# Head sums sent through DRAM and divided feature-major, and a norm in groups of 4 tiles, in a macaron transformer block

## What is computed

```
x = x + 0.5 * ffn(layernorm(x))
x = x + attn(layernorm(x))
x = x + 0.5 * ffn(layernorm(x))
# attn: q, k, v = split(x @ w_qkv.T), 16 heads of 16
probs = softmax(where(causal, q @ k.T / 4, lowest))
out = (probs @ v), heads side by side -> out @ w_out.T
# ffn: softmax of the gate over the tokens, top 2 of 8,
#      y = relu chain of w1, w2, w3; v[e] = sum of y * weight; out = chosen @ v
```

## Time and profile before

| what | before |
|---|---|
| median of 3 runs | 2114.99 us |
| lowest, highest | 2114.93 us, 2117.0 us |
| the profiled execution, its own time | 2126.23 us |
| its span in the profile | 2124.5 us |
| PE busy | 2047.7 us (96%) |
| PE's weight loads busy | 1584.0 us (75%) |
| DVE busy | 1817.7 us (86%) |
| ACT busy | 1598.6 us (75%) |
| POOL busy | 414.5 us (20%) |

### The profile page before, as it was taken

The page is one execution under the profiler, slowest core; times in us unless marked ns, Lnnn a source line. Parts: engine busy times, 40 slices in busy tenths (PEclk is TensorE's granted clock), DMA queues, the critical chain, the costliest instruction groups (busy, mean ns, idle before and its releaser), DMA issues.

```text
span 2124.5 us, 99858 instructions
## 1 busy us (share of the span) xinstructions
PE 2047.7 (96%) x43659; PEld 1584.0 (75%) x43659; DVE 1817.7 (86%) x4023; ACT 1598.6 (75%) x3311; POOL 414.5 (20%) x1118
## 2 busy tenths in 40 slices
PE   5899989999999999999999999999999999879998
PEld 3788866377877777777787777777778776658885
DVE  6666666899999999999999999999999994676665
ACT  5344446599999999999999999999999998334442
POOL 1333213411121111121111111111111111023330
PEclk8899989999999999999999999999999999979998
DMA  8211103300010000100001001000010002231112
GB/s 273 74 47 50 42 16 125 134 30 25 13 34 14 25 30 8 34 20 18 31 7 33 22 16 34 9 29 27 11 34 16 22 4 69 54 118 47 45 49 88
DMA packets 70394, 94.36 MB, mean 44 GB/s; under 512 B 16640, under 2 KB 59396, under 8 KB 69956
## 3 DMA queue, kind: packets, MB, share of 16 engines
q1 hardware_dynamic: 62796, 68.75, 10.1%
q0 software_dynamic: 6816, 19.20, 3.4%
q10 hardware_dynamic: 344, 0.01, 0.0%
HBM read 62.24 MB, written 25.43 MB: 41 GB/s over the span
## 4 chain that ended last, share of the span: by engine, by line
PE 88%; DVE 6%; issue 2%; ACT 1%; POOL 1%; DMA 1%; SPq 1%; another core or an unknown queue 0%; DVEq 0%; ACTq 0%; POOLq 0%
PE bank L1264 39%; PE bank L1257 22%; PE bank L1139 17%; PE bank L1346 3%; PE bank L1150 1%; PE bank L1375 1%; DVE stats L1405 1%; PE bank L1307 1%; PE bank L1157 1%; DVE rows L1427 1%; DVE x_res L1725 1%; SPq L698 0%; POOL work L591 0%; DVE work L1594 0%; PE bank L1217 0%
## 5 line engine op out<-in xcount | busy, mean ns | idle before, releaser
L966 ACT ACTIVATE feat<-bank 128x512 f32<-128x512 f32 (+3 forms) x2304 | 1263.2, 565 | 113.8 <-PE bank L1264 13.3
L1264 PE MATMUL bank<-work 96*32 96x512 bf16 (+2 forms) x15872 | 1206.4, 370 | 5.0 <-DVE work L1772 3.8
L1772 DVE TENSOR_REDUCE work<-bank 128x1 f32<-128x512 f32 (+1 forms) x1920 | 1178.9, 659 | 26.4 <-PE bank L1264 23.4
L1257 PE MATMUL bank<-feat,phase 128*17 128x128 f32 (+3 forms) x18432 | 879.2, 263 | 0.3 <-ACT feat L972 0.3
L1257 PEld LDWEIGHTS bank<-feat,phase 128*17 128x17 f32 x18432 | 588.4, 98 | 270.7 <-ACT feat L972 13.7
L1264 PEld LDWEIGHTS bank<-work 96*32 96x32 bf16 (+1 forms) x15872 | 472.6, 96 | 57.1 <-DVE work L1772 24.6
L1139 PE MATMUL bank<-work 128*128 128x256 f32 (+1 forms) x1872 | 398.4, 363 | 0.6 <-issue 0.2
L1139 PEld LDWEIGHTS bank<-work 128*128 128x128 f32 x1872 | 325.1, 192 | 37.1 <-issue 1.0
L625 POOL TENSOR_SCALAR_AFFINE_SELECT feat<-feat 128x128 f32<-128x128 f32 x512 | 145.1, 292 | 456.0 <-ACT feat L966 439.1
L1656 DVE COPY work<-phase 128x514 f32 x234 | 101.5, 436 | 124.1 <-ACT work L880 99.5
L578 POOL DMA_INDIRECT work<-token_table,row_no x142 | 138.1, 973 | 299.0 <-PE bank L1150 142.6
(11 more groups left out here) (201 smaller groups left out, 1371.9 us busy)
## 6 DMA issues: line engine op xcount, KB each, us to landing
phase<-in_w SPq DMA_DIRECT2D x12, 1024.0 KB, 12.0
work<-qk_parts SPq DMA_DIRECT2D x60, 192.0 KB
token_table<-rows SPq DMA_DIRECT2D x8, 1056.0 KB, 8.7
work<-work SPq DMA_DIRECT2D x512, 0.5 KB
qk_parts<-phase SPq DMA_DIRECT2D x20, 384.0 KB, 2.8
work<-qk_parts SPq DMA_DIRECT2D x60, 128.0 KB
qk_parts<-work SPq DMA_DIRECT2D x12, 384.0 KB, 2.8
x_res<-in_x SPq DMA_DIRECT2D x8, 512.0 KB
```

What stands on the lines that cost most here:

```text
L966: eng.activation(p_ring[:, n % P_RING, lo:QB], s_bank("probs", n)[:, lo:QB], ACT.Exp, scale=HD ** -0.5).then_inc(sig.s_done, 1)
L1257: mm = eng.matmul(bank[ACC_BANK][GRID * g:GRID * g + VW, GRID * i0:P], v_aug[:, t, h, :], weights[:, i0:TPJ, g, :], start=(t == 0), stop=( ...
L1264: mm = eng.matmul(out[GRID * g:GRID * (g + 1), width], left[:, GRID * g:GRID * (g + 1)], right, start=start, stop=stop)
L1772: eng.tensor_reduce(maxima[:, h % 2, j, PLACE[i], at:at + 1], scores[:, 0:hi - lo], AX_X, ALU.max).then_inc(sig.a_done, 1)
```

## The change

What ACT copied out of the PSUM bank is no longer transposed by DVE. SP stores it in DRAM (`head_sums`, [head, row, token]). When 8 heads of a query block are there (heads 7 and 15), five steps follow: SP loads the sums of 8 heads by 512 tokens as 128 by 32 ("load_totals"), DVE takes their reciprocals, SP stores them and loads both the 128 features by 512 tokens and the reciprocals, each spread over its head's 16 rows ("load_parts"), and DVE multiplies 128 by 512 ("divide"). `heads` is now feature-major, as the projection wants it, so the transpositions of heads (L1359) and ACT's copies (L980) are gone. The norm behind attention goes in groups of 4 tiles instead of 8. For the last unit, reciprocals and divide stand inside the projection's loop. The input's tokens are ordered otherwise on the host, and ACT's copies of the norm before attention undo that. The rows of the third norm lie in `work` instead of `rows`, the one-hot tensors of the second routing in `rows`, and three waits move: the load of the experts' weights waits for the last division, `acc` for the store of two units ago, and the staging of weights for the second table's store.

```diff
-LN_GRP = (4, 4, GRP)
+LN_GRP = (4, 4, 4)
...
+HEADS_PER_PART = P // HD
+TOTALS = HEADS_PER_PART * QB // P
...
-PV_LAG, PV_PAUSE, TURN_LAG, DIVIDE_LAG = 5, 1, 2, 2
+PV_LAG, PV_PAUSE, STORE_LAG = 5, 1, 2
+LAST_RECIPROCALS, LAST_DIVIDE = 8, 16
+DIVIDE_STEPS = (("load_totals", 7), ("reciprocals", 14), ("store_reciprocals", 16), ("load_parts", 21), ("divide", 30))
...
-        while unturned and unturned[0][0] <= n:
-            yield "turn", unturned[0][1]
-            undivided.append((n + DIVIDE_LAG, unturned.pop(0)[1]))
...
-                unturned.append((n + TURN_LAG, h * NJ + j))
+                later.append((n + STORE_LAG, "store_sums", h * NJ + j))
+                if h % HEADS_PER_PART == HEADS_PER_PART - 1:
+                    later += [(n + lag, what, h * NJ + j) for what, lag in DIVIDE_STEPS]
+                later.sort()
...
-        while undivided and undivided[0][0] <= n:
-            yield "divide", undivided.pop(0)[1]
+        while later and later[0][0] <= n:
+            yield later.pop(0)[1:]
...
+        sums_dram = nc.dram_tensor("head_sums", (H, GRID, S), F32).ap()
+        recips_dram = nc.dram_tensor("head_reciprocals", (H, S), F32).ap()
...
-        heads = rows[:, :, 0:D]
+        heads = rows[:, :, :].rearrange("p i r -> p (i r)")[:, 0:KD * S].rearrange("p (k s) -> p k s", k=KD)
+        late_rows = work[:, 0:NT * ROW].rearrange("p (i r) -> p i r", i=NT)
+        def rows_of(f):
+            return late_rows if f else rows
+        def summed_of(h, j):
+            return heads[:, h // HEADS_PER_PART, j * QB:(j + 1) * QB]
+        def recips_of(h, j):
+            return recips[j] if h // HEADS_PER_PART else heads[:, 1, j * QB:(j + 1) * QB]
+        def units_of(h, j):
+            return slice(h - HEADS_PER_PART + 1, h + 1), slice(j * QB, (j + 1) * QB)
+        def divisions(h, j):
+            return h // HEADS_PER_PART * NJ + j + 1
+        def of_parity(h, j):
+            return h // HEADS_PER_PART * NJ // 2 + j // 2 + 1
...
-                    elif what == "divide":
-                        h, j = UNITS[n]
-                        need.wait_ge(sig.recip, n + 1)
-                        eng.tensor_tensor(heads[:, TPJ * j:TPJ * (j + 1), h * HD:(h + 1) * HD], sums[:, n % 2, :, 0:HD],
-                                          bc(recip[:, n % 2, :], 2, [P, TPJ, HD]), ALU.mult).then_inc(sig.divided, 1)
...
                 if f == 1:
                     need.wait_ge(sig.pv, PV_ALL)
+                    need.wait_ge(sig.divided, KD * NJ)
...
+                elif what == "store_sums":
+                    h, j = UNITS[n]
+                    need.wait_ge(sig.acc, n + 1)
+                    eng.dma_start(sums_dram[h, :, j * QB:(j + 1) * QB].rearrange("w (g c) -> g w c", g=TPJ),
+                                  acc_out[:, n % 2, :]).then_inc(sig.sums_stored[n % 2], 16)
+                elif what == "load_totals":
+                    h, j = UNITS[n]
+                    heads_of, tokens = units_of(h, j)
+                    need.wait_ge(sig.sums_stored[n % 2], 16 * (n // 2 + 1))
+                    eng.dma_start(totals[:, j % 2, :], sums_dram[heads_of, HD, tokens]).then_inc(sig.totals_loaded[j % 2], 16)
+                elif what == "store_reciprocals":
+                    h, j = UNITS[n]
+                    heads_of, tokens = units_of(h, j)
+                    need.wait_ge(sig.recip, divisions(h, j))
+                    eng.dma_start(recips_dram[heads_of, tokens], totals[:, j % 2, :]).then_inc(sig.recips_stored[j % 2], 16)
+                elif what == "load_parts":
+                    h, j = UNITS[n]
+                    heads_of, tokens = units_of(h, j)
+                    need.wait_ge(sig.recips_stored[j % 2], 16 * of_parity(h, j))
+                    if h >= HEADS_PER_PART:
+                        need.wait_ge(sig.divided, divisions(h - HEADS_PER_PART, j))
+                    eng.dma_start(summed_of(h, j), sums_dram[heads_of, 0:HD, tokens]).then_inc(sig.parts_loaded[j % 2], 16)
+                    eng.dma_start(recips_of(h, j), recips_dram[heads_of, tokens].unsqueeze(1).to_broadcast(
+                        [HEADS_PER_PART, HD, QB])).then_inc(sig.parts_loaded[j % 2], 16)
...
-                        eng.activation(feat[:, k, i0 * P:(i0 + 4) * P], bank[k][:, :],
-                                       ACT.Copy).then_inc(sig.feat[n], 1)
+                        to, of = feat[:, k, i0 * P:(i0 + 4) * P], bank[k][:, :]
+                        if n == 1:
+                            to = to.rearrange("p (i g b) -> p g i b", i=TPJ, g=TPJ)
+                            of = of.rearrange("p (g i b) -> p g i b", i=TPJ, g=TPJ)
+                        eng.activation(to, of, ACT.Copy).then_inc(sig.feat[n], 1)
...
-                        need.wait_ge(sig.turned, n - 1)
+                        need.wait_ge(sig.sums_stored[n % 2], 16 * (n // 2))
...
-            def copy_heads(n):
-                need.wait_ge(sig.pv, PV_ALL)
-                need.wait_ge(sig.s_full, S_ALL)
-                for k in range(KD):
-                    m = n * KD + k
-                    need.wait_ge(sig.heads_tr, 4 * (m + 1))
-                    eng.activation(feat[:, k, 4 * n * P:4 * (n + 1) * P], bank[H_BANKS[m % len(H_BANKS)]][:, :],
...
-            def transpose_heads(n):
-                need.wait_ge(sig.a_done, len(A_ITEMS))
-                need.wait_ge(sig.divided, len(UNITS))
-                for k in range(KD):
-                    m = n * KD + k
-                    need.wait_ge(sig.heads_copy, m - len(H_BANKS) + 1)
-                    for i in range(4 * n, 4 * n + 4):
-                        eng.transpose(bank[H_BANKS[m % len(H_BANKS)]][:, (i - 4 * n) * P:(i - 4 * n + 1) * P],
-                                      rows[:, i, k * P:(k + 1) * P], ident[:, :]).then_inc(sig.heads_tr, 1)
-
             def attended(g):
-                for n in range(2 * g, 2 * g + 2):
-                    if n == 0:
-                        transpose_heads(0)
-                    if n + 1 < NT // 4:
-                        transpose_heads(n + 1)
-                    for i2 in range(4 * n, 4 * n + 4, 2):
-                        need.wait_ge(sig.heads_copy, KD * (n + 1))
-                        need.wait_ge(sig.acc, len(UNITS))
-                        need.wait_ge(sig.attended, i2 // 2 - 1)
-                        bk = 4 + i2 // 2 % 2
-                        for i in (i2, i2 + 1):
-                            for k in range(KD):
-                                eng.matmul(bank[bk][:, (i - i2) * D:(i - i2 + 1) * D], feat[:, k, i * P:(i + 1) * P],
-                                           w_out_sb[:, k, :], start=(k == 0),
-                                           stop=(k == KD - 1)).then_inc(sig.out_mm, 1)
+                for i2 in range(g * LN_GRP[2], (g + 1) * LN_GRP[2], 2):
+                    need.wait_ge(sig.divided, divisions(H - 1, i2 // TPJ))
+                    need.wait_ge(sig.a_done, len(A_ITEMS))
+                    need.wait_ge(sig.acc, len(UNITS))
+                    need.wait_ge(sig.attended, i2 // 2 - 1)
+                    bk = 4 + i2 // 2 % 2
+                    for i in (i2, i2 + 1):
+                        for k in range(KD):
+                            eng.matmul(bank[bk][:, (i - i2) * D:(i - i2 + 1) * D], heads[:, k, i * P:(i + 1) * P],
+                                       w_out_sb[:, k, :], start=(k == 0),
+                                       stop=(k == KD - 1)).then_inc(sig.out_mm, 1)
...
-                    need.wait_ge(sig.heads_tr, 4 * KD * 2 * (g + 1))
+                    need.wait_ge(sig.s_full, S_ALL)
                 for i in range(a, b):
-                    eng.tensor_scalar(rows[:, i, 0:D], x_res[:, i, :], mean_var[:, i, 0:1], rstd[:, 0, i:i + 1],
+                    eng.tensor_scalar(rows_of(n // 2)[:, i, 0:D], x_res[:, i, :], mean_var[:, i, 0:1], rstd[:, 0, i:i + 1],
...
+                if f == 1:
+                    need.wait_ge(sig.table[f], 16 * GROUPS)
...
-                for i2 in range(g * GRP, (g + 1) * GRP, 2):
+                for i2 in range(g * LN_GRP[2], (g + 1) * LN_GRP[2], 2):
                     need.wait_ge(sig.out_mm, KD * (i2 + 2))
                     add_pair(i2, 4 + i2 // 2 % 2, sig.attended)
+                    if i2 + 2 == LAST_RECIPROCALS:
+                        reciprocals(*UNITS[-1])
+                    if i2 + 2 == LAST_DIVIDE:
+                        divide(*UNITS[-1])
+            def reciprocals(h, j):
+                need.wait_ge(sig.totals_loaded[j % 2], 16 * of_parity(h, j))
+                eng.reciprocal(totals[:, j % 2, :], totals[:, j % 2, :]).then_inc(sig.recip, 1)
+            def divide(h, j):
+                need.wait_ge(sig.parts_loaded[j % 2], 32 * of_parity(h, j))
+                eng.tensor_tensor(summed_of(h, j), summed_of(h, j), recips_of(h, j), ALU.mult).then_inc(sig.divided, 1)
...
-                    elif what == "turn":
-                        need.wait_ge(sig.acc, n + 1)
```

(13 more changed lines are left out.)

87 lines of the change are left out of this document (37 added, 50 removed).

## The result

The changed kernel takes **2146.1 us** (median of 4 runs, 2145.06 to 2147.25) where the kernel before took 2115.87 beside it: a ratio of **1.0144**, with a 95% interval from 1.0129 to 1.0159. It is slower by some 30 us; forecast was 2095, and faster. The profiled execution of the change took 2146.41 us, 0.3 above its median, with a span of 2144.7; that of before was 11.24 us above its own.

The account below looks back on a forecast made before the run. PE was taken as the bound in attention, DVE close behind; behind attention no engine is full. Terms -10 + 1 - 4.4 - 6.6 = -20 us took the median from 2114.99 to 2095 us, range 2086 to 2108.

Parts of the forecast that it names:

- The chain of transfers: In attention, SP's added stores and loads for the division: 16 divisions under 0.1 us each, +1 us (0 to 6).
- the first and the third leg: From storing sums to loading totals, and storing reciprocals to loading parts: 3.0 us slack against 3.4, holding SP 0.4 us.
- three banks: Scores between DVE and PE in attention, 3 x 0.6 us, taken to cover 1.8 us of each DVE stop.
- a rival behind attention: Norm's groups of 4 run at a low PE clock, 8 x 1.7 = 14 us more: 2109 us, chance 0.08.
- the division chain comes late, and DVE stops in line: Rival, inside attention: legs of 6.8 us instead of 3.4, 30 stops costing PE 0.8 us each: 2119 us, chance 0.09.
- DVE's relief in attention: In attention, fewer DVE transpositions and reciprocals shorten PE's waits for DVE: -10 us (0 to 25 us gained).
- attention gives nothing: Rival: PE's matmuls already fill attention, so relieving DVE gains nothing there and only the end remains: 2105 us, chance 0.14.
- the last rival: In attention, DVE was worth more: all 24.9 us of waits shrink by two thirds, -17 instead of -10: 2088 us, chance 0.07.
- The start of the projection: Behind attention, the last copy lets PE start projecting at once, without turn, reciprocal, product and first transposition: -4.4 us.
- The norm in groups of 4: Behind attention, DVE and PE each need about 5.25 us a group, 48.8 us instead of 56.1: -6.6 us taken.
- Behind it: After the norm, experts' weights and table stores arrive in time; routing moves earlier and keeps its length: 0 us.
- The product beside POOL: In attention, each DVE product could stand behind one POOL selection of 0.29 us: 4.4 us, time 2099.4 instead of 2095.

Follow-up runs that it names:

- e9: The change with head 7's divisions spread, each unit's 60 items later than the one before, short lags kept: 2146.03 us, ratio 1.01 to the kernel before.
- e12: The change with heads 7 and 8's loads of the next stack cut into transfers of 16 rows outermost, same bytes: 2141.81 us, ratio 1.0078.
- e10: The change without DVE's reciprocals and products of head 7, all of SP's transfers kept: 2133.37 us, ratio 1.0039.
- e1: The change with heads 0 to 7's divisions spread 60 items apart and longer lags (20 to 84 items), head 15 unchanged: 2108.76 us, ratio 0.9967.
- e3: The change with the norm behind attention in groups of 8 tiles again: 2155.14 us, ratio 1.0187.
- e4: The kernel before the change with only the norm behind attention in groups of 4 tiles: 2113.69 us, ratio 0.9986.
- e5: The change with longer lags in head 7 (11, 22, 24, 33, 42 items), divisions as close together as before: 2137.34 us, ratio 1.006.

## Why the prediction was wrong, point by point

*The chain of transfers, forecast +1 us, was +38 in heads 7 and 8 and +2.5 in head 15.* This step failed, in three places.

First, the leg. I took 2.8 us from one row, a median over stores issued elsewhere in the program, plus 0.6, and called it 3.4 for every leg. Measured in head 7, the store of sums took 5.9 to 7.8 us and that of the reciprocals 5.3 (7.5 in e9), each against a slack of 3.0; the load of parts took 4.95, against 5.4, and was late only because it was issued late. The size of the transfer had little to do with it: in head 15, where no stack is loaded, 16 KB of reciprocals are issued at 1796.90 and SP goes on at 1798.78, 1.9 us later:

```profile
1796.90 0.61 SPq L764 DMA_DIRECT2D head_reciprocals<-work  x1
1798.78 0.61 SPq L771 DMA_DIRECT2D rows<-head_sums  x1
```

The price was set by what had been issued ahead in SP's queue. Loads of the stack whose outermost dimension is 3 or 2 are a large part: with 16 outermost (e12) the legs are 3.1 and 3.4 us, which is what I had assumed. Ahead of the store that took 7.8 us stood two loads of 256 KB as well. I had costed each leg as if it were alone. The rule of the Trainium skill that I put beside this rival (DMA: Bandwidth & Descriptors, "Specifications": transfers under 512 bytes become a read-modify-write) is not needed for it: these reciprocals are stored in pieces of 128 bytes, and took 1.9 us in one place and 7.5 in another.

Second, the line on SP. I wrote that the first and the third leg could hold SP for 0.4 us "where nothing is due at once". SP was held for 7.2 us at 1043.02 (and for 4.7 at 1035.73), and due behind it were the next loads of totals and parts, which DVE then waited for, and rows of maxima that PE needs. The change's trace shows the first of these at work; e10, without DVE's waits, shows the second, at 16.7 us for the two heads.

Third, what a stop costs. I subtracted three banks, 1.8 us, from each stop. DVE's waits for DMAs in the two heads, 31.3 us in nine places, became 25.3 us of idle PE: 0.7 us a stop was covered, and of the stop of 4.84 us only 0.2. And PE's granted clock fell to 0.50 four times in these heads, at 1045.4, 1110.2, 1130.7 and 1158.0, in or just behind stops of PE of 4.65, 2.18, 3.99 and 5.06 us; a stop of 2.67 us, at 1036.89, had no such fall. The longest stretch (the granted clock is the number ahead of the DMA share):

```profile
1045.40:1059.00 13.60, 7.67 (x96) 3.43 (x96) 4.81 (x10) 3.26 (x6) 0.00 (x0) 0.50 0.24 76
```

PE's matmuls took 12.8 us longer in the two heads, a third of the loss; half of the 22.05 us that PE was busy at 0.50 are 11.0 of it. I had this effect as a rival behind attention only the earlier trace rows.

*The rival "the division chain comes late, and DVE stops in line" happened,* with a chance of 0.09. Its place and its sign were right. Its point (each leg 3.4 us longer than assumed, 6.8) was reached by some stores (7.5 and 7.8 us) and not by others (5.3 and 5.9) nor by the load of parts (4.95), and still the time is 27 us above its 2119. It counted 30 stops of 0.8 us; there were nine, with 2.8 us of idle PE each, and it knew nothing of what SP's own waits delay or of the clock. Its evidence against was bad: the DMA share of 0.07 says how little is moved, as a mean over 16 DMA engines, and nothing about how long one transfer waits for another on the few it runs on. Two rows were there to be read: SP's own queue in a head, where pieces of the stack come one after another, and the share in a short stretch of one of them, 0.19 (under e12), where the mean over attention has 0.07.

*DVE's relief in attention, forecast -10 us, was 0.* This step failed too. Heads without a division take 86.7 us, as before, though DVE has some 37 / 16 = 2.3 us less to do in each. PE was busy for 1377.45 of 1379 us; the weight loads' waits for DVE did not move the matmuls, and most of them could go without a gain. This is the rival "attention gives nothing", and with e1 its time can be read: 2105 was written for it, and e1, the change with its legs repaired, gives 0.9967 x 2114.99 = 2108. (The 24.9 us that the last rival takes from the earlier trace rows should read 25.0; nothing hangs on it.)

*The start of the projection, -4.4 us:* right. 0.4 us from the start of the last copy to PE, where it had been 4.8 (1794.25 to 1799.01): -4.3.

*The norm in groups of 4, -6.6 us:* right in kind, a little small. Forecast were 5.25 us a group and 48.8 us for the course; measured 5.0 on DVE, 5.3 on PE, and 48.3, so -7.8 in the profile, and 9 us by e3. In the kernel before it is 3 us (e4).

*Behind it, 0:* from the first maximum of routing to the end it is 265.4 us in the change and 265.1 in e1. The profile of before has 269.4, but e4, which has before's code there, has 265.2; the 4 us belonged to that one execution.

*The product beside POOL:* in the trace of the change one product starts beside the last of three selections, and takes 0.80 us instead of the median of 0.69:

```profile
1829.33 0.82 POOL L659 TENSOR_SCALAR_AFFINE_SELECT feat<-feat 128x128 f32<-128x128 f32 x3
...
1829.89 0.80 DVE L1767 TENSOR_TENSOR rows<-rows,phase 128x512 f32<-128x512 f32 x1 [7.28 <-DMA phase<-head_reciprocals]
```

By the Trainium skill (SBUF — State Buffer, "SBUF: two separate sides") I had put a whole selection, 0.29 us, on each product. The row shows 0.11 us in the length of the product; whether its start was held as well can't be seen behind its wait for the DMA. e1's heads with eight products take 86.7 to 86.9 us, so they show no cost.

The sum with measured terms: 38.1 + 2.5 in attention, -4.3 for the start, -7.8 for the norm: +28.5, where the medians say +30.2. The last 1.7 us I don't place; single runs of the change are up to 2.2 us apart. The two profiled spans are only 20.2 us apart, because that execution of before was 4.4 us later when head 7 began (1021.25 against 1016.89; e5, with the change's code up to there, has 1021.16) and took the 3.9 us more behind routing's first maximum.

## What to carry to other kernels

Before a chain of small transfers goes into an in-order queue, write down for each leg what is issued ahead of it in that queue, and for each wait on the issuing engine what is queued behind it; a mean DMA share answers neither. Look at the outermost dimension of the large transfers in that queue first: 3 or 2 there made small ones behind them wait. Slack is cheap to buy (here more items of lag and a tile per unit instead of two), but it takes much of it: legs of 5.4 to 6.6 us (e5) gave half of the loss back, and legs of 12 us with the divisions 60 items apart (e1) turned +1.4% into -0.3%. And a wait of a weight load is not a wait of the matmuls: where PE's matmuls already fill the stretch, relieving the engine they wait for brings nothing.

## What the runs showed of the hardware that I had not expected

A 16 KB store to DRAM was done 1.9 us after its issue with an empty queue, 7.5 us with two loads of the stack (192 KB each) and a 64 KB store issued in the 2.2 us ahead of it (e9), and 3.4 us behind one load of the stack cut into parts of 16 rows (e12), where it was 5.3 us in the change. A load of 192 KB with 3 outermost kept 0.19 of the 16 DMA engines busy and moved 66 GB/s; with 16 outermost it was 0.54 and 148 GB/s. The reciprocal of 128x32 took 344 ns, where 128x4 took 158 and I had assumed 200. And the granted clock fell in attention at PE's stops, of 2.18 to 5.06 us in the change: the mean over head 7 is 0.92 in the change with 16.0 us of idle PE, 0.97 in e5 with 7.3 us, and 1.00 in e1 with none.
